# GNN setup stage: tile tables turned on TensorE and stored in one transfer, input loaded behind the weights, norms by ScalarE inside the projection

## Chip, cores and metric

One core of one Trainium2 chip. The metric is the device time of the kernel in microseconds (us), the median of the runs shown. Numbers of the profile come from one profiled execution.

## The reference

A graph network over 6,250 nodes with 128 features and 106,250 edges sorted by destination. Four layers follow each other, each with a LayerNorm and a ReLU ahead of it and a residual sum behind it. What matters here is the opening of layer 0:

```
h = relu(layer_norm(x))                        # 6250 x 128
q = typed_linear(h, node_type, Wq)             # one of 3 weight matrices per node
k = typed_linear(h, node_type, Wk) @ rel_att   # per head
v = typed_linear(h, node_type, Wv) @ rel_msg   # per head
attention over each node's incoming edges, weights exp(a - max) / sum
```

The later layers gather rows per edge and sum them per destination node (a mean, a gated sum, a mean again), and all four use the same table of edge tiles.

## The kernel before

**Tiles.** The edges, sorted by destination, are cut into T = 896 tiles of 128 (NC = 7 columns of 128 tiles each), each tile for one block of 128 nodes; the nodes fill 49 blocks, padded to NS = 50. For every tile three integers are needed later: its node block, its first edge, and the key of its last edge. They are worked out on VectorE (DVE) with tile number = partition + 128 x column and sit as three int32 arrays of 128 partitions x 7 words (`bI`, `sI`, `kI`, in OUTDEG). They go to a DRAM table `metad` of 3 x 896 words, tile after tile, and are read back from it as rows by several later loads.

**Setup, up to the projection.**

- SyncE (SP) issues the loads: one column of destinations (L834), the whole input X of 3.2 MB (L835), then 13 weight and parameter loads (L847). They are on one queue in this order.
- DVE finds the row of destinations in which each block boundary falls; GpSimd (POOL) gathers these rows (L707, 128 rows of 831 words) and DVE waits for them before L1496.
- DVE counts, ranks the blocks (L1501 to L1537), works out which tile belongs to which block (L1540 to L1561), and signals POOL, which gathers 7 source windows and 7 destination windows (L715, 14 gathers).
- DVE works out the order of turns (L1563 to L1585), masks of the node types (L1593 to L1598), copies the combined K and V weights from PSUM to W3 (L1602, L1603) and adds the FiLM row (L1604).
- DVE takes the moments of X in 50 blocks (L1404) and the factors of the norm (`spread`, L1408 to L1421, with a square root on ScalarE, ACT). Then `normalise` writes H = relu(norm(X)): 21 of the 50 blocks on ACT (L1116), 29 on DVE (L1428) with one ReLU over them (L1432). DVE waits for ACT's (L1611), then casts the gathered windows (L1614 to L1616).

**The projection** (`pe_proj`, `act_proj`, `dve_proj`, `sp_proj` with n = 0) is a pipeline over the 50 blocks. For block b DVE multiplies H by the three type masks (L532), TensorE (PE) turns the three products (L499), ACT copies them out of PSUM (L517), PE multiplies them with W3 (L506), DVE writes the queries to QT (L559) and keys and values to a staging tile STG of two slots (L526), and SP stores the slot to the table `tab2` (L592). DVE may write a slot again only when the store of two blocks earlier has landed. `pairs` (L244) lays out the steps: the first `lead` pairs of blocks and the last pair are written out, those between are a loop over a register. With n = 0 the lead is PLAN_LEAD = 15 pairs, so that blocks 0 to 29 are written out.

Other work is hung onto written-out blocks. DVE's `plan(b)` (L1618) builds the edge tables in blocks 1 to 13; PE turns 14 tiles at block 5 (L493). SP stores these tables from block 16 on, two more transfers at each of 8 blocks (`sp_tiles`, L568), then at block 24 the three arrays of `metad` (L586):

```
for k, values in ((2, kI), (0, bI), (1, sI)):
    sp.dma_start(metad[k, :].rearrange("(c p) -> p c", p=P), values)...
```

At block 28 SP waits for all of them (`tiles_stored`, STORES = 16 x 21) and loads BROW back from `metad`. POOL waits for the same count before it loads the flags (L723, L724, L727) and clears ACCR (L728). When the last store to `tab2` has landed, POOL starts the 3,520 row gathers (L691) that feed all four layers.

Of the kernel before, what the change touches and what calls it, by code (L numbers as in the profile page):

```python
# [7 lines left out]
I32 = mybir.dt.int32  # L8
# [4 lines left out]
P = 128  # L13
# [57 lines left out]
def build(nc, sz, a):  # L71
# [4 lines left out]
    with ctx:  # L76
# [167 lines left out]
        def pairs(eng, fn, trailing, lead=2):  # L244

            n = NS // 2
            for r in range(2 * lead):
                fn(r, r % 2)
            if n > lead + 1:
                with eng.Fori(lead, n - 1) as i:  # L250
                    for r in range(2):
                        fn(i * 2 + r, r)
            for r in range(2):
                fn(NS - 2 + r, r)
            for r in range(trailing):
                fn(NS + r, r)
# [94 lines left out]
        KEYS_KNOWN, WINDOWS_KNOWN, TURNS_KNOWN, SIG_IN, FILM_IN, TILES_KNOWN, TILES_MASKED = range(1, 8)  # L351
        TOTALS, ORDER_KNOWN, W_COMBINED, TILES_TURNED = range(1, 5)
# [19 lines left out]
        exp_out = sem("exp_out")  # L372
        w_free = sem("w_free")
# [10 lines left out]
        STORES = 16 * (5 + 2 * ROWS_OF)  # L384
# [29 lines left out]
        ON_ACT = (NS * 21 // 50, NS * 3 // 5, NS * 21 // 50)  # L414
# [15 lines left out]
        bI, sI, kI = (OUTDEG[:, k * NC:(k + 1) * NC].bitcast(I32) for k in range(3))  # L430
# [41 lines left out]
        PLAN_TURNED, PLAN_STORED, PLAN_LOADED = 5, 16, 28  # L472
        PLAN_LEAD = (PLAN_LOADED + 2) // 2
        TILE_ROWS = PSA[:, :, :, :].rearrange("p r j d -> p (r j d)").rearrange("p (k e) -> p k e", k=2)

# [7 lines left out]
        def pe_proj(pe, n):  # L483
# [4 lines left out]
            def step(b, r):  # L488
                if n == 0 and isinstance(b, int) and b == PLAN_TURNED:
# [4 lines left out]
                    last.then_inc(reckoned, 1)  # L494
                if has_block(b):
# [15 lines left out]
        def act_proj(act, n):  # L511
# [7 lines left out]
            pairs(act, step, 0, PLAN_LEAD if n == 0 else 2)  # L519

        def dve_proj(dve, n, plan=None):
# [457 lines left out]
        def _(pe):  # L979
# [15 lines left out]

            pe_proj(pe, 0)
# [103 lines left out]
        def _(act):  # L1100
# [68 lines left out]
            normalise(X, H, ACT.Relu)  # L1169
            act_proj(act, 0)  # L1170
# [200 lines left out]
        def _(dve):  # L1371
# [122 lines left out]

            dve.wait_ge(dst_loaded, 16)
# [24 lines left out]
            c(v_.tensor_copy(pIf, pI))  # L1520
# [19 lines left out]
            c(v_.tensor_scalar(p15, pI, GROUP - 1, None, ALU.bitwise_and))  # L1540
            c(v_.tensor_scalar(p4, pI, 4, None, ALU.logical_shift_right))
            c(v_.tensor_copy(p15f, p15))
            c(v_.tensor_copy(p4f, p4))
            c(v_.tensor_copy(grp, cI))
            c(v_.tensor_scalar(grp, grp, p4f, None, ALU.add))
            c(v_.tensor_scalar(tp, p15f, float(sz.chunk), None, ALU.mult))
            c(v_.tensor_scalar(tpos, grp, tp, None, ALU.add))
            c(v_.tensor_copy(partI, grp))
            c(v_.tensor_scalar(partI, partI, sz.chunk.bit_length() - 1, None, ALU.logical_shift_right))
            c(v_.tensor_copy(off, partI))  # L1550
            c(v_.scalar_tensor_tensor(tpos, off, float((GROUP - 1) * sz.chunk), tpos, ALU.mult, ALU.add))
# [7 lines left out]
            c(v_.tensor_copy(bI, bt))  # L1559
# [42 lines left out]
            c(v_.tensor_copy(W3[:, :, 0:D], PB[1][:, 0:3 * D].rearrange("p (t d) -> p t d", t=3)))  # L1602
# [400 lines left out]
```

## Time and profile before

| | us |
|---|---|
| median of 3 runs (5033.28 to 5042.1) | 5039.2 |
| profiled execution, its own time | 5043.33 |
| span of the profiled execution | 5041.3 |
| PE busy / DVE busy / ACT busy / POOL busy | 3019.7 / 3090.2 / 1498.2 / 3399.2 |

The span holds everything between the first and the last instruction; 2.0 us of the profiled execution lie around it. Busy times are sums over the engine's instructions. In the rows further down "L592" is line 592 of the kernel, SPq and POOLq are the queues from which these engines issue transfers, and what stands behind an arrow in brackets is what ended the idle time before an instruction.

### The profile page before, as it was taken

The numbers are of one execution on the slowest core, as the hardware profiler recorded it, in microseconds if no ns is written. First come the engines' busy times: TensorE is split into PE (matmuls) and PEld (weight loads), VectorE is DVE, ScalarE is ACT, GpSimd is POOL, SyncE is SP. The second block draws the span as 40 slices with busy tenths as digits, with TensorE's granted clock in tenths as the row PEclk, the third lists the DMA queues.
The fourth block names the chain that finished last, engine by engine and source line by source line (L and its number), as shares of the span: only waits on it lengthen the run. The fifth ranks groups of instructions, "written<-read, shape, count | busy, mean of one in ns | idle before, by whom it ended". The sixth has DMA issues, their size and how long they took to land.

```text
span 5041.3 us, 77470 instructions
## 1 busy us (share of the span) xinstructions
PE 3019.7 (60%) x15685; PEld 2533.8 (50%) x15686; DVE 3090.2 (61%) x8230; ACT 1498.2 (30%) x2837; POOL 3399.2 (67%) x3564
## 2 busy tenths in 40 slices
PE   5645555555563444455555999999996444444443
PEld 3435555454553444444443777777775434433443
DVE  6377777777777666645553777777775444444443
ACT  1123333333312000011112666666663122222222
POOL 1477777777502777777774777777774777777775
PEclk8767777777776555567775999999998555555555
DMA  2568777787811222222225767766766222222224
GB/s 75 107 171 233 226 233 224 226 230 229 209 50 45 53 53 53 53 60 66 65 66 71 189 189 185 188 186 186 187 185 106 56 56 56 56 56 56 56 56 41
DMA packets 536616, 616.11 MB, mean 122 GB/s; under 512 B 98148, under 2 KB 420751, under 8 KB 536432
## 3 DMA queue, kind: packets, MB, share of 16 engines
q0 software_dynamic: 142256, 349.44, 27.5%
q1 hardware_dynamic: 394176, 264.70, 19.8%
q14 instruction: 129, 1.06, 0.1%
q8 instruction: 55, 0.90, 0.1%
HBM read 529.54 MB, written 84.25 MB: 122 GB/s over the span
## 4 chain that ended last, share of the span: by engine, by line
POOL 43%; issue 20%; DMA 15%; DVE 10%; PE 7%; DVEq 2%; ACT 2%; SPq 1%; POOLq 0%; ACTq 0%
POOL G L691 43%; DMA G<-tab,SRC 9%; DMA mvd<-G 3%; DVE ACCR L1398 2%; PE PB L506 2%; PE PSA L902 1%; PE PB L1088 1%; DVEq L650 1%; DMA MV<-mvd 1%; PE PB L499 1%; PE PB L1026 1%; DVE ACCR L1886 1%; DMA tab<-G 1%; DVE FLG L1868 1%; ACT PB L1244 0%
## 5 line engine op out<-in xcount | busy, mean ns | idle before, releaser
L691 POOL DMA_INDIRECT G<-tab,SRC x3520 | 3360.6, 955 | 1374.1 <-issue 1042.1
L1398 DVE TENSOR_TENSOR ACCR<-ACCR,PSA 128x128 f32 (+2 forms) x3536 | 1126.9, 319 | 750.8 <-PE PSA L902 388.8
L902 PE MATMUL PSA<-G,S 128*128 128x128 f32 x3520 | 861.2, 421 | 1153.1 <-DMA G<-tab,SRC 949.2
L902 PEld LDWEIGHTS PSA<-G,S 128*128 128x128 f32 x3520 | 739.7, 311 | 1263.8 <-DVE ACCR L1398 699.7
L1381 DVE TENSOR_TENSOR S<-PB,REL 128x512 f32<-128x512 f32 x884 | 606.0, 686 | 38.3 <-DVE MASK L1450 13.7
L1026 PE MATMUL PB<-QTR,ST 128*128 x1792 | 341.3, 351 | 300.1 <-ACT ST L1207 162.3
L1026 PEld LDWEIGHTS PB<-QTR,ST 128*128 128x128 f32 x1792 | 299.9, 253 | 335.5 <-issue 334.5
L902 PE MATMUL PSA<-FLG,S 128*128 128x256 f32 x1760 | 421.8, 383 | 2.8 <-DVE FLG L1868 2.7
L902 PEld LDWEIGHTS PSA<-FLG,S 128*128 128x128 f32 x1760 | 337.3, 192 | 146.5 <-issue 91.7
L902 PE MATMUL PSA<-SCR,S 128*128 128x137 f32 x1792 | 330.7, 342 | 18.6 <-DVE ACCR L1398 18.6
L902 PEld LDWEIGHTS PSA<-SCR,S 128*128 128x128 f32 x1792 | 307.3, 248 | 23.3 <-DVE SCR L1777 23.3
L1088 PE MATMUL PB<-G,ident 128*128 128x512 f32 x440 | 245.8, 641 | 96.3 <-DMA G<-tab,SRC 86.9
L1204 ACT ACTIVATE S<-S,small 128x512 bf16<-128x512 bf16 x224 | 161.2, 720 | 372.2 <-DMA S<-relt 371.9
L1080 PEld LDWEIGHTS PB<-W,SCR 128*128 128x128 f32 x1760 | 233.1, 193 | 34.8 <-DMA SCR<-in_ea_t 22.5
L1080 PE MATMUL PB<-W,SCR 128*128 128x128 f32 x1760 | 234.1, 276 | 21.8 <-DMA SCR<-in_ea_t 21.8
L1084 PE MATMUL PB<-QTR,ST 128*128 x1760 | 234.0, 276 | 0.0
L1770 DVE TENSOR_TENSOR SCR<-G,PB 128x512 f32<-128x512 f32 x224 | 152.9, 683 | 107.7 <-issue 57.3
L1084 PEld LDWEIGHTS PB<-QTR,ST 128*128 128x128 f32 x1760 | 215.8, 193 | 0.0
L1868 DVE TENSOR_TENSOR FLG<-G,PB 128x512 f32<-128x512 f32 x220 | 149.6, 680 | 102.1 <-ACT PB L1244 98.9
L1920 DVE TENSOR_TENSOR X<-X,SCR 128x128 f32 x57 | 17.2, 302 | 310.9 <-ACT SCR L1283 310.9
L1242 ACT ACTIVATE FLG<-PB 128x512 f32<-128x512 f32 x220 | 130.2, 592 | 254.4 <-PE PB L1088 253.8
L1777 DVE TENSOR_TENSOR SCR<-MV,SCR 128x512 f32<-128x512 f32 x224 | 154.4, 689 | 75.5 <-DMA MV<-mvd 75.3
(317 smaller groups left out, 3693.0 us busy)
## 6 DMA issues: line engine op xcount, KB each, us to landing
mvd<-G SPq DMA_DIRECT2D x224, 256.0 KB, 3.4
MV<-mvd SPq DMA_DIRECT2D x224, 256.0 KB, 5.1
G<-tab,SRC POOLq DMA_INDIRECT x3520, 2.5
SCR<-in_ea_t SPq DMA_DIRECT2D x880, 64.0 KB
S<-relt SPq DMA_DIRECT2D x224, 128.0 KB
SCR<-reld SPq DMA_DIRECT2D x220, 128.0 KB
tab<-SCR SPq DMA_DIRECT2D x57, 128.0 KB, 1.7
tab<-G SPq DMA_DIRECT2D x50, 128.0 KB, 1.7
```

The source lines that it names most:

```text
L691: nc.gpsimd.indirect_dma_start(out=rows[:, slot, j, :], out_offset=None, in_=table, in_offset=bass.IndirectOffsetOnAxis(ap=SRC[:, k:k + 1] ...
L902: last = nc.tensor.matmul((PSA if banks is None else banks)[:, par, j, 0:width], S[:, slot, j, :], rhs(j), start=True, stop=True)
L1026: last = nc.tensor.matmul(QD[v % 2][:, j, :], ST[:, v % 2, j, :], QT[:, bass.ds(blocks[j], 1), :].rearrange("p o d -> p (o d)"), start=Tru ...
L1080: nc.tensor.matmul(QD[v % 2][:, j, :], EA[:, slot, j, :], W[:, 4 * D:5 * D], start=j == 0, stop=False, skip_group_check=True)
L1084: nc.tensor.matmul(QD[v % 2][:, j, :], ST[:, v % 2, j, :], QT[:, bass.ds(blocks[j], 1), :].rearrange("p o d -> p (o d)"), start=False, sto ...
L1088: nc.tensor.matmul(QD[v % 2], ident[:, :], G2[:, slot, :, 0:D], start=False, stop=True, skip_group_check=True).then_inc(s["pre_done"], 1)
L1204: nc.scalar.activation(far, far, ACT.Square, bias=minus_p).then_inc(s["far_known"], 1)
L1381: return v_.tensor_tensor(S[:, slot, :, :], bc(IOTAP, [P, QUAD, P], 1), REL[:, bass.ds(q * QUAD, QUAD)].unsqueeze(2).to_broadcast([P, QUAD ...
L1398: v_.tensor_tensor(rows, rows, banks[:, par, j, 0:width], ALU.add).then_inc(s["rows_added"], 1)
L1770: v_.tensor_tensor(PROD[:, v % 2, :, :], G2[:, slot, :, 0:D], QD[v % 2], ALU.mult).then_inc(s["multiplied"], 1)
L1777: v_.tensor_tensor(WM[:, mv % 2, :, 0:D].rearrange("p j (h d) -> p j h d", h=HEADS), MV[:, mslot, :, :].rearrange("p j (h d) -> p j h d", ...
L1868: v_.tensor_tensor(RHS[:, v % 2, :, 0:D], G2[:, slot, :, D:2 * D], GATEP, ALU.mult).then_inc(s["multiplied"], 1)
```

## The change

1. SP: the load of X moves from the front to behind the 13 loads of L847.
2. DVE: twelve small instructions on tile numbers (L1540 to L1551) and one cast (L1520) move up, to between the signal `row_known` (L1493) and the wait for the gathered rows (L1495).
3. The block and first edge of each tile are written as floats to META = ACCR[:, 576:597]; `sI` is still written as integers as well (it gives the window numbers), `bI` and `kI` are not. The key goes to META in block 9. At block 16 PE multiplies META (as the weights, 128 x 21) with the identity, which turns it to 21 rows of 128; at block 19 DVE casts them to integers in METAI (21 partitions x 128); at block 24 SP waits for that and stores it in one transfer.
4. The copies of the combined weights to W3 move from DVE to ACT, and PE waits for them ahead of the projection.
5. `normalise` is not called for layer 0's input. ACT norms four blocks ahead of the projection, and block b + 4 behind its copy of block b in each step; DVE waits for the norm of block b before L532. DVE's part of the norms, its ReLU and its wait for ACT are gone. ACT writes out the last two pairs of steps and not one.

```diff
-        def pairs(eng, fn, trailing, lead=2):
+        def pairs(eng, fn, trailing, lead=2, tail=1):
...
-        STORES = 16 * (5 + 2 * ROWS_OF)
+        STORES = 16 * (3 + 2 * ROWS_OF)
...
-        ON_ACT = (NS * 21 // 50, NS * 3 // 5, NS * 21 // 50)
+        ON_ACT = (NS, NS * 3 // 5, NS * 21 // 50)
...
-        bI, sI, kI = (OUTDEG[:, k * NC:(k + 1) * NC].bitcast(I32) for k in range(3))
+        sI = OUTDEG[:, NC:2 * NC].bitcast(I32)
+        META = ACCR[:, 576:576 + 3 * NC]
+        METAI = ACCR[0:3 * NC, 640:640 + P].bitcast(I32)
...
+        AHEAD = 4
+        META_ROWS = TILE_ROWS[0:3 * NC, 0, T:T + P]
...
+                if n == 0 and isinstance(b, int) and b == PLAN_META:
+                    pe.wait_ge(planned, TILES_MASKED)
+                    nc.tensor.matmul(META_ROWS, META, ident[:, :], start=True, stop=True).then_inc(reckoned, 1)
...
+                if n == 0 and has_block(b + AHEAD):
+                    ahead(b + AHEAD)
+            if n == 0:
+                for b in range(AHEAD):
+                    ahead(b)
+                pairs(act, step, 0, PLAN_LEAD, AHEAD // 2)
...
                 if has_block(b) and n == 0:
+                    dve.wait_ge(normed, b + 1)
...
                 if isinstance(b, int) and b == PLAN_STORED + ROWS_OF:
-                    for k, values in ((2, kI), (0, bI), (1, sI)):
-                        sp.dma_start(metad[k, :].rearrange("(c p) -> p c", p=P), values).then_inc(tiles_stored, 16)
+                    sp.wait_ge(planned, META_KNOWN)
+                    sp.dma_start(metad.rearrange("k (c p) -> (k c) p", p=P), METAI).then_inc(tiles_stored, 16)
...
-            sp.dma_start(X[:, :, :], a["x"].rearrange("(b p) d -> p b d", p=P)).then_inc(x_loaded, 16)
...
                 for dst, src in loads:
                     sp.dma_start(dst, src).then_inc(w_loaded, 16)
+                sp.dma_start(X[:, :, :], a["x"].rearrange("(b p) d -> p b d", p=P)).then_inc(x_loaded, 16)
...
+            pe.wait_ge(w_made, 2)
             pe_proj(pe, 0)
...
             nc.scalar.activation(SIG[:, 0:3], SKIP[:, 0:3], ACT.Sigmoid).then_inc(sig_out, 1)
-            normalise(X, H, ACT.Relu)
-            act_proj(act, 0)
+            act.wait_ge(reckoned, W_COMBINED)
+            for k in range(2):
+                nc.scalar.copy(W3[:, :, k * D:(k + 1) * D], PB[1 + k][:, 0:3 * D].rearrange("p (t d) -> p t d", t=3)).then_inc(w_made, 1)
+            root(st2)
+            turn_no[0] += 1
+            act.wait_ge(factors_known, turn_no[0])
+
+            def norm_row(b):
+                line = lambda tab: tab[:, bass.ds(b, 1), 0:D].rearrange("p o d -> p (o d)")
+                nc.scalar.activation(line(H), line(X), ACT.Relu, bias=st1[:, bass.ds(b, 1)],
+                                     scale=st2[:, bass.ds(b, 1)]).then_inc(normed, 1)
+            act_proj(act, 0, norm_row)
...
+            c(v_.tensor_copy(pIf, pI))
+            c(v_.tensor_scalar(p15, pI, GROUP - 1, None, ALU.bitwise_and))
...
+            c(v_.scalar_tensor_tensor(tpos, off, float((GROUP - 1) * sz.chunk), tpos, ALU.mult, ALU.add))
+
             dve.wait_ge(dst_loaded, 16)
...
-            c(v_.tensor_copy(bI, bt))
+            c(v_.tensor_copy(META[:, 0:NC], bt))
+            c(v_.tensor_copy(META[:, NC:2 * NC], st))
             c(v_.tensor_copy(sI, st))
...
             moments(X, range(NS))
             spread()
-            normalise(X, H)
-            dve.wait_ge(normed, NORMED[1])
-
             dve.wait_ge(windows_in, 32 * NC)
...
-                    c(v_.tensor_copy(kI.unsqueeze(2), KEYW[:, :, P - 1:P]))
+                    c(v_.tensor_copy(META[:, 2 * NC:3 * NC].unsqueeze(2), KEYW[:, :, P - 1:P]))
...
+                if b == 19:
+                    dve.wait_ge(reckoned, META_TURNED)
+                    c(v_.tensor_copy(METAI, META_ROWS))
+                    dve.sem_inc(planned, 1)
```

## Rows read from the trace of the kernel before

**Rows 1.** The page: span, and the chain that ended last by engine

```profile
span 5041.3 us, 77470 instructions
POOL 43%; issue 20%; DMA 15%; DVE 10%; PE 7%; DVEq 2%; ACT 2%; SPq 1%; POOLq 0%; ACTq 0%
```

**Rows 2.** Timeline of SP, POOL and DVE, 0 to 20 us: start, duration, instruction

```profile
1.35 0.94 SPq L835 DMA_DIRECT2D X<-in_x  x1
2.34 10.69 SPq L847 DMA_DIRECT2D S<-in_wk_t  x1
6.02 1.11 POOL L707 DMA_INDIRECT G<-in_dst_pm,QTR  x1 [4.18 <-DVEq L1493]
13.94 0.59 DVE L1496 CAST G<-G 128x831 f32<-128x831 int32 x1 [8.26 <-DMA G<-in_dst_pm,QTR]
...
19.51 0.44 SPq L847 DMA_DIRECT2D ROWS<-in_film_b  x1
```

**Rows 3.** Window gathers of L715: times from issue to landing

```profile
DMA to landing us min/median/max: 2.4/3.8/7.7
```

**Rows 4.** Timeline of DVE, ACT and POOL, 25 to 66 us

```profile
25.22 0.15 DVE L1540 TENSOR_SCALAR QTR<-QTR 128x1 int32<-128x1 int32 x1
...
27.71 0.52 DVE L1552 TENSOR_TENSOR QTR<-QTR 128x350 f32<-128x350 f32 x1
...
39.22 0.56 DVE L1602 COPY W<-PB 128x384 f32<-128x384 f32 x1
...
40.41 0.42 DVE L1604 TENSOR_TENSOR ROWS<-ROWS,PB 128x256 f32<-128x256 f32 x1
40.86 9.76 DVE L1404 BATCH_NORM_STATS2 ACCR<-X 128x6 f32<-128x128 f32 x50
...
48.62 0.94 POOL L715 DMA_INDIRECT G<-in_dst_win,QTR  x1 [0.30 <-issue]
...
53.38 8.18 ACT L1116 ACTIVATE H<-X,st 128x128 f32<-128x128 f32 x21 [0.84 <-DVEq L1421]
53.44 7.52 DVE L1428 TENSOR_SCALAR H<-X,st 128x128 f32<-128x128 f32 x29 [0.15 <-DVE st L1420]
...
63.12 0.63 DVE L1614 CAST SCR<-G 128x896 f32<-128x896 int32 x1
...
65.23 1.03 DVE L532 TENSOR_TENSOR G<-H,MASK 128x384 f32<-128x384 f32 x2 [0.15 <-DVE ACCR L1616]
```

**Rows 5.** Timeline of the projection, 126 to 156 us

```profile
126.03 1.73 SPq L587 DMA_DIRECT2D metad<-OUTDEG  x3
...
129.66 2.10 PE L506 MATMUL PB<-W,G 128*128 128x384 f32 x6
...
131.92 2.10 PE L506 MATMUL PB<-W,G 128*128 128x384 f32 x6
...
148.57 0.42 DVE L526 TENSOR_SCALAR G<-PB 128x256 f32<-128x256 f32 x1 [16.48 <-DMA tab<-G]
...
153.81 2.10 PE L506 MATMUL PB<-W,G 128*128 128x384 f32 x6
```

**Rows 6.** The three stores of L587: issue to landing

```profile
DMA to landing us min/median/max: 10.4/20.5/21.2
```

**Rows 7.** Transfers issued up to 330 us: size, median us to landing

```profile
reld<-G SPq DMA_DIRECT2D x8, 28.0 KB, 1.9
```

**Rows 8.** Stretch 131 to 149 us: engines' busy time, PEclk, DMA share, GB/s

```profile
131.00:149.00 18.00, 3.02 (x12) 1.56 (x10) 0.72 (x3) 0.48 (x1) 0.35 (x1) 0.73 0.91 13
```

**Rows 9.** Waits up to 290 us: total, times, longest

```profile
POOL G L691 <- DMA tab<-G: 36.1, 1, 36.1
...
DVE G L526 <- DMA tab<-G: 18.8, 3, 16.5
```

**Rows 10.** Instruction groups of ACT up to 290 us: busy, mean ns, idle before

```profile
L517 ACT COPY G<-PB 128x384 f32<-128x384 f32 x50 | 24.0, 480 | 113.1 <-PE PB L499 113.1
...
L1108 ACT ACT_TABLE_LOAD x1 | 1.3, 1283 | 0.0
```

More of the change, by code:

```diff
@@ L248, in pairs @@
                 fn(r, r % 2)
-            if n > lead + 1:
-                with eng.Fori(lead, n - 1) as i:
+            if n > lead + tail:
+                with eng.Fori(lead, n - tail) as i:
                     for r in range(2):
                         fn(i * 2 + r, r)
-            for r in range(2):
-                fn(NS - 2 + r, r)
+            for r in range(2 * tail):
+                fn(NS - 2 * tail + r, r % 2)
             for r in range(trailing):
@@ L350, in build @@
         windows_in = sem("windows_in")
-        KEYS_KNOWN, WINDOWS_KNOWN, TURNS_KNOWN, SIG_IN, FILM_IN, TILES_KNOWN, TILES_MASKED = range(1, 8)
-        TOTALS, ORDER_KNOWN, W_COMBINED, TILES_TURNED = range(1, 5)
+        KEYS_KNOWN, WINDOWS_KNOWN, TURNS_KNOWN, SIG_IN, FILM_IN, TILES_KNOWN, TILES_MASKED, META_KNOWN = range(1, 9)
+        TOTALS, ORDER_KNOWN, W_COMBINED, TILES_TURNED, META_TURNED = range(1, 6)
         turns_in = sem("turns_in")
@@ L372, in build @@
         exp_out = sem("exp_out")
+        w_made = sem("w_made")
         w_free = sem("w_free")
@@ L470, in proj_sems @@
             return s
-        PLAN_TURNED, PLAN_STORED, PLAN_LOADED = 5, 16, 28
+        PLAN_TURNED, PLAN_META, PLAN_STORED, PLAN_LOADED = 5, 16, 16, 28
         PLAN_LEAD = (PLAN_LOADED + 2) // 2
         TILE_ROWS = PSA[:, :, :, :].rearrange("p r j d -> p (r j d)").rearrange("p (k e) -> p k e", k=2)
+        AHEAD = 4
+        META_ROWS = TILE_ROWS[0:3 * NC, 0, T:T + P]
         proj = [proj_sems(n) for n in ("typed_qkv", "typed_out")]
@@ L509, in pe_proj, with act_proj @@
             pairs(pe, step, 1, PLAN_LEAD if n == 0 else 2)
-        def act_proj(act, n):
+        def act_proj(act, n, ahead=None):
             s, (ni, w, cols) = proj[n], proj_w[n]
@@ L518, in step @@
                                PB[r][:, 0:ni * P]).then_inc(s["copied"], 1)
-            pairs(act, step, 0, PLAN_LEAD if n == 0 else 2)
+                if n == 0 and has_block(b + AHEAD):
[4 more added lines that the diff above has]
+                pairs(act, step, 0, PLAN_LEAD, AHEAD // 2)
+            else:
+                pairs(act, step, 0)
         def dve_proj(dve, n, plan=None):
@@ L1493, in _ @@
             dve.sem_inc(row_known, 1)
+            c(v_.tensor_copy(pIf, pI))
+            c(v_.tensor_scalar(p15, pI, GROUP - 1, None, ALU.bitwise_and))
+            c(v_.tensor_scalar(p4, pI, 4, None, ALU.logical_shift_right))
+            c(v_.tensor_copy(p15f, p15))
+            c(v_.tensor_copy(p4f, p4))
+            c(v_.tensor_copy(grp, cI))
+            c(v_.tensor_scalar(grp, grp, p4f, None, ALU.add))
+            c(v_.tensor_scalar(tp, p15f, float(sz.chunk), None, ALU.mult))
+            c(v_.tensor_scalar(tpos, grp, tp, None, ALU.add))
+            c(v_.tensor_copy(partI, grp))
+            c(v_.tensor_scalar(partI, partI, sz.chunk.bit_length() - 1, None, ALU.logical_shift_right))
+            c(v_.tensor_copy(off, partI))
+            c(v_.scalar_tensor_tensor(tpos, off, float((GROUP - 1) * sz.chunk), tpos, ALU.mult, ALU.add))
             dve.wait_ge(dst_loaded, 16)
@@ L1537, in _ @@
             c(v_.tensor_tensor(delta[:, 1:NE], rel0[:, 1:NE], rel0[:, 0:NE - 1], ALU.subtract))
[L1540 to L1551, printed above, removed]
             c(v_.tensor_tensor(M, bc(cum, [P, NC, NE], 1), tpos.unsqueeze(2).to_broadcast([P, NC, NE]), ALU.is_le))
@@ L1601, in _ @@
             dve.wait_ge(reckoned, W_COMBINED)
-            c(v_.tensor_copy(W3[:, :, 0:D], PB[1][:, 0:3 * D].rearrange("p (t d) -> p t d", t=3)))
-            c(v_.tensor_copy(W3[:, :, D:2 * D], PB[2][:, 0:3 * D].rearrange("p (t d) -> p t d", t=3)))
             c(v_.tensor_tensor(ROWS[:, 3:5, :].rearrange("p a d -> p (a d)"), ROWS[:, 3:5, :].rearrange("p a d -> p (a d)"),
```

1 line of the change is left out of this document (removed).

## Prediction

> **What bounds the kernel now.** I read the page first, for the size of things: over the span of 5041.3 us the chain that ended last is mostly POOL [rows 1], the row gathers of the four layers, and the change touches none of them. So the question is when the first of these gathers can start, and whether what follows merely moves with it. POOL is ready long before: it sits idle for 36.1 us until the last store to the table has landed [rows 9]. The end of the projection sets it, and behind that lies one serial path, which I then followed in the timeline. It has three pieces. (1) DVE's stream from the boundary rows to the first masked block, 65.23 us [rows 4], nearly without a gap but for 8.26 us in which it waits for the gathered rows [rows 2]. (2) The projection at PE's pace: two neighbouring steps start at 129.66 and 131.92, 2.26 us apart [rows 5]. (3) A hole in it: DVE cannot refill a staging slot for 16.48 us, until 148.57, since a store to the table has not landed [rows 5].
>
> What the hole waits for is seen from two sides. The three stores of L587 took 10.4 to 21.2 us to land [rows 6], though they carry 3.5 KB each, while a store of 28 KB from the same queue takes 1.9 us [rows 7]. In that stretch the transfer engines are busy for 0.91 of the time and move 13 GB/s [rows 8]: 2,688 single words, one after the other, with the table's stores queued behind them.
>
> **The change part by part.** Durations and sum refer to the profiled execution, 5043.33 us with 2.0 us around its span; it is 4.1 us above the median of 5039.2, and I take the same difference off both.
>
> *X behind the weights.* Today X (3.2 MB) is in flight from 1.35 us, the first weight load is held in issue for 10.69 us, and the last is issued at 19.51 [rows 2]. The gather of boundary rows, issued at 6.02, lands 7.9 us later among this traffic. With X last, the weights take some 8 us to issue (the other twelve took 13.03 to 19.95 us, and the first should be like its neighbour), so that X leaves at about 9.5 us, when the gather is nearly in. The window gathers, of a sixth of the size, took 2.4 to 7.7 us, 3.8 at the median [rows 3]. These are my ends: below by 2.4, above by the present 7.9. I take 4.5 (the median, and something for the size): DVE goes on at 10.5 and not 13.94, minus 3.4 us. X itself needed 15.6 us at most of flight and would be in by 25 us; DVE asks for it at about 34. It costs nothing; with that cover gone, each us later than 34 would cost one.
>
> *Thirteen instructions moved up.* L1540 to L1551 take from 25.22 to 27.71 [rows 4], 2.5 us, and L1520 one more step of 0.2: 2.7 us leave the chain. In their new place they run from 5.8 to 8.5 us, inside the wait for the gather. This is also a floor: however fast the gather is, DVE does not go on before 8.5, so the first term can be 5.4 at most. One more copy (first edges both as float and as integer) costs 0.2. Net minus 2.5.
>
> *W3 copied by ACT.* L1602 to L1604 start 1.19 us apart [rows 4]: minus 1.2. ACT has nothing else to do then, and PE needs W3 only at the projection, some 15 us later.
>
> *Norms.* With 7.1 us saved so far the moments start at 33.8 and the factors are ready at 46.4 (53.44 before). From there to L1614 at 63.12 is 9.7 us of norm, ReLU and wait [rows 4], which leave DVE's path. What is late next is the windows: their gathers start 5.9 us earlier (they do not profit from the W3 copies), so the last is issued at 42.7 and not 48.62 [rows 4] and lands, at the median of 3.8 [rows 3], at 46.5. DVE's casts thus start at 46.5 or 46.6. ACT's four norms ahead take 4 x 0.39 us (21 in 8.18 [rows 4]), 1.6 us, beside DVE's casts of 2.1. The first masked block comes at 48.7 and not 65.23: **minus 16.5** for all parts together up to here. The ends are minus 12 (gather unchanged, windows 1 us late) and minus 18.5.
>
> Inside the projection ACT has 2.26 us a step, of which its copy takes 0.48 [rows 10]. A norm of 0.48 brings it to 0.96. The norm stands behind the copy that PE waits for and four blocks ahead of its use. Cost zero, hidden in ACT's idle time. What the register addresses of the 16 rolled steps cost on ACT no row shows: below nothing is excluded, above it is free up to the slack of 1.3 us a step. I take 0.
>
> Here a rule speaks against the change. DVE does 29 blocks in 7.52 us with 2.1 for their ReLU, 0.33 a block, and ACT 0.39 [rows 4]; ACT is the slower engine for it. The Trainium skill (ScalarE: Activation LUTs, Rules for kernel authors) says to put ReLU and multiplications on VectorE and not on ScalarE. By it, 50 blocks ahead of the loop would cost 19.5 us of ACT against 9.7 now; that this kernel places all but four under PE's steps is what the rule leaves out.
>
> *One store in place of three.* The hole: from 131.92 to 153.81 PE gets two steps done in 21.89 us, where 4.53 are due. It costs 17.4 us [rows 5], of which 16 are the wait and the rest PE restarting at a lower clock (0.73 granted in the stretch [rows 8]). The 2,688 words become 21 rows of 512 bytes. I price their landing by the 28 KB store, 1.9 us [rows 7], no more than the other stores of these blocks, which stop nobody. Added is one turn on PE, the engine that sets the pace: six passes of 384 columns take 2.10 us [rows 5], 0.35 each, so two passes of 128 columns cost between 0.1 and 0.7, I take 0.4; and one cast on DVE, hidden in its wait for PE. SP's new wait at block 24 has only table stores behind it, and DVE signals in block 19: nothing. What stays is the flags' traffic: of DVE's three waits on the table's stores (18.8 us) the other two are 2.3 [rows 9]. POOL will issue these loads earlier, but as before inside the projection, so I leave them as they are; they may cost up to 3 us more or 1 less. **Minus 17.0.**
>
> *Sum:* 16.5 + 17.0 = 33.5. 5043.3 becomes 5009.8 in a profiled execution, and the median 5039.2 becomes 5005.7. Everything behind the projection starts 33.5 us earlier and depends on nothing with a time of its own: POOL will have cleared its flags and ACCR some 36 us ahead of need, as now.
>
> **The rivals.**
>
> *The hole stays.* If the table's stores were held not by the single words but by the backlog of the 17 transfers of blocks 16 to 23, or the flags' loads took the place of the words, some 16.5 us remain: 5022. For it speaks only that these come together; against it, that each of the 28 KB stores landed in 1.9 us until the single words came. 5 in 100.
>
> *No change.* Layer 0 could be paced by something that does not move, and take back what is given. The wait of 36.1 us [rows 9] says that POOL hangs on the table alone. Time 5035 to 5043. 4 in 100.
>
> *Slower, by ACT's tables.* ReLU and copy now alternate on ACT, 50 times. If each change of function needed a table, at 1283 ns a load [rows 10], a step would take 0.96 + 2 x 1.28 = 3.5 us of ACT, over PE's 2.26: 50 x 1.25 = 62 us lost, 33 gained, 5068. The point at which this turns to a loss is 2.93 us a step. Against it: in the first 290 us, where 21 ReLUs are followed by 50 copies, the square root's table is the only one loaded after the sigmoid's [rows 10]. The Trainium skill (ScalarE: Activation LUTs, Table sets) says that relu and copy are in every set; its price for a switch, about 2.7 us, would give 120 us more. 2 in 100.
>
> **How the numbers follow.** 0.2%, about 10 us, is what a measurement can tell from no change. The forecast has 88 in 100, the rivals 5, 4 and 2, one is left for a loss of another kind. Within the forecast the ends are minus 12 and minus 18.5 for the first part, minus 13.5 and minus 18 for the second, and the runs themselves spread over 9 us: 5006 becomes 4996 to 5018. I take the upper end to 5020. Faster 0.93, same 0.04, slower 0.03.
>
> **What would show it.** L1496 at 10 to 11 us, L1404 at about 34, L1614 at 46 to 47 with windows or DVE as its releaser, the first L532 at 48.7. ACT's steps with a copy and a norm, no table load between. The store to metad landing in about 2 us, PE's steps 2.26 us apart through blocks 24 to 30, no wait of L526 over 3 us, the first L691 at 171 to 173. The forecast is wrong if the first L691 is later than 180, or if it is not, and the span is still less than 25 us shorter.

## The result, and the profile after

The changed kernel takes 5006.8 us, the median of 4 runs (5003.98 to 5009.44). The kernel before takes 5039.4 us beside it (5033.28 to 5042.1). The ratio is 0.9933 with an interval of 0.9918 to 0.9948, 32.6 us less. The profiled execution took 5007.18 us around a span of 5005.4.

First the page, to see whether anything changed behind the setup. Span and chain:

```profile
span 5005.4 us, 77541 instructions
POOL 44%; issue 20%; DMA 15%; DVE 9%; PE 7%; DVEq 2%; ACT 2%; SPq 1%; POOLq 0%; ACTq 0%
```

The chain is the one of [rows 1], 35.9 us shorter. So I followed the serial path again. The timeline of SP, POOL, DVE and ACT, 6 to 51 us (start, duration, instruction, idle time before it and what ended it):

```profile
6.02 1.11 POOL L724 DMA_INDIRECT G<-in_dst_pm,QTR  x1 [4.19 <-DVEq L1521]
...
8.15 0.87 SPq L864 DMA_DIRECT2D X<-in_x  x1
...
8.48 0.17 DVE L1535 SCALAR_TENSOR_TENSOR QTR<-ACCR,QTR 128x7 f32<-128x7 f32 x1
12.74 0.59 DVE L1538 CAST G<-G 128x831 f32<-128x831 int32 x1 [4.09 <-DMA G<-in_dst_pm,QTR]
...
36.03 9.76 DVE L1432 BATCH_NORM_STATS2 ACCR<-X 128x6 f32<-128x128 f32 x50
...
44.98 0.94 POOL L732 DMA_INDIRECT G<-in_dst_win,QTR  x1 [0.30 <-issue]
...
48.56 1.65 ACT L1196 ACTIVATE H<-X,st 128x128 f32<-128x128 f32 x4 [0.84 <-DVEq L1449]
48.61 0.63 DVE L1639 CAST SCR<-G 128x896 f32<-128x896 int32 x1
...
50.71 1.03 DVE L549 TENSOR_TENSOR G<-H,MASK 128x384 f32<-128x384 f32 x2 [0.15 <-DVE ACCR L1641]
```

Against [rows 2, 4]: DVE goes on behind the gather at 12.74 (13.94 before), starts the moments at 36.03 (40.86), casts the windows at 48.61 (63.12) and makes the first masked block at 50.71 (65.23). The part up to there is 14.5 us shorter. Two details count later. The small instructions end at 8.65 and DVE still waits 4.09 us for the gather. And no bracket stands behind L1639: the windows were there, DVE itself was the last to arrive.

Then the projection, in the timeline of PE, DVE, SP and POOL from 90 to 129 us, and POOL's first row gather:

```profile
90.46 0.40 PE L503 MATMUL PSA<-ident,ACCR 128*21 128x128 f32 x2
...
112.45 0.38 SPq L604 DMA_DIRECT2D metad<-ACCR  x1
...
114.15 0.64 POOL L740 DMA_DIRECT2D FLG<-flagd  x1 [68.23 <-DMA metad<-ACCR]
...
116.09 2.10 PE L515 MATMUL PB<-W,G 128*128 128x384 f32 x6
...
118.35 2.10 PE L515 MATMUL PB<-W,G 128*128 128x384 f32 x6
...
125.16 2.10 PE L515 MATMUL PB<-W,G 128*128 128x384 f32 x6
...
127.17 0.42 DVE L542 TENSOR_SCALAR G<-PB 128x256 f32<-128x256 f32 x1 [1.74 <-DMA tab<-G]
...
128.90 2.10 PE L515 MATMUL PB<-W,G 128*128 128x384 f32 x6
...
174.68 1.03 POOL L708 DMA_INDIRECT G<-tab,SRC  x1 [39.98 <-DMA tab<-G]
```

The hole of [rows 5] is gone. The store to `metad` is issued at 112.45, and at 114.15 POOL passes its wait for it: it landed in 1.7 us at most, where the three stores took 10.4 to 21.2 [rows 6]. PE's steps stay 2.26 us apart (116.09, 118.35), but for one pair, 125.16 to 128.90, 1.48 us over the pace. The first row gather starts at 174.68 and not 205.26: 30.6 us earlier.

ACT's groups up to 290 us (busy, mean ns, idle before):

```profile
L1196 ACT ACTIVATE H<-X,st 128x128 f32<-128x128 f32 (+1 forms) x50 | 24.4, 494 | 0.8 <-DVEq L1449 0.8
...
L526 ACT COPY G<-PB 128x384 f32<-128x384 f32 x50 | 24.0, 479 | 76.0 <-PE PB L508 76.0
...
L1126 ACT ACT_TABLE_LOAD x1 | 1.3, 1283 | 0.0
```

POOL still waits for the table alone, 39.98 us before its first row gather. ACT does all 50 norms and idles 76.0 us over the 50 copies (113.1 in [rows 10]). ACT changes from copy to ReLU and back fifty times, and no further table load appears. DVE waits for stores to the table four times, 2.9 us in all, the longest 1.7 (three times and 18.8 in [rows 9]).

### The profile page after: what moved, and what is told of

Read it like the earlier page. It is cut to its first block, busy times and chain, and to the rows that moved or that the text cites. A ratio compares the mean times of both kernels' runs of the same rounds, so it can differ in the third digit from the quotient of the medians.

```text
span 5005.4 us, 77541 instructions
## 1 busy us (share of the span) xinstructions
PE 3026.9 (60%) x15687; PEld 2538.2 (51%) x15688; DVE 3080.3 (62%) x8200; ACT 1509.9 (30%) x2868; POOL 3394.4 (68%) x3564
## 4 chain that ended last, share of the span: by engine, by line
POOL 44%; issue 20%; DMA 15%; DVE 9%; PE 7%; DVEq 2%; ACT 2%; SPq 1%; POOLq 0%; ACTq 0%
POOL G L708 44%; DMA G<-tab,SRC 10%; DMA mvd<-G 3%; DVE ACCR L1426 3%; PE PB L515 2%; PE PSA L919 1%; PE PB L1106 1%; DVEq L667 1%; PE PB L508 1%; DVE ACCR L1915 1%; DMA MV<-mvd 1%; SPq L791 1%; DVE FLG L1897 1%; ACT PB L1272 0%; ACT L1143 0%
```

## The experiments

Three things were to be found out: whether the parts of the change add up as the sum says; what holds the gather of boundary rows, which was far from the forecast; and how near ACT is to setting the pace. The kernels ran in three groups of four, each group on one chip and beside the kernel before on that chip. I compare the time from the start of the span to the first row gather of layer 0, and the median against that of the kernel before in the same group. The kernel before was only timed in the groups: its first row gather is always the 205.26 us of its own profile, and that of the changed kernel the 174.68 above, but for the third group. The totals named in the expectations start from 5039 us, and the kernel before is 7.7 us faster on the first group's chip; so for the totals I compare differences. "The first chip" is the one of the changed kernel's own runs; its trace is the one read above.

### First group: the parts alone (before: 5031.7 us, 16 runs, 5026.88 to 5035.3)

**Words.** The three columns are stored as single words again, everything else is as changed:

```diff
-                    sp.wait_ge(planned, META_KNOWN)
-                    sp.dma_start(metad.rearrange("k (c p) -> (k c) p", p=P), METAI).then_inc(tiles_stored, 16)
+                    for k, values in ((2, kI), (0, bI), (1, sI)):
+                        sp.dma_start(metad[k, :].rearrange("(c p) -> p c", p=P), values).then_inc(tiles_stored, 16)
```

> The changed kernel with the three stores of single words put back (no turn on PE, no METAI). Theory (the words hold the table's stores behind them): DVE waits some 16 us for a staging slot around block 24, the first row gather of layer 0 starts 16 to 18 us later than in the changed kernel (174.7 there), near 191.5, and the whole time rises by as much, to about 5023. Rival (the backlog of the 17 other transfers is the cause): the wait is as short as in the changed kernel and the time moves by less than 3 us.

Measured: first row gather at 190.0 us, 15.3 later than with the change; median 5018.4 (5016.79 to 5028.45), ratio 0.9977 (0.9967 to 0.9987). The wait and its length, in the waits and in the timeline:

```profile
DVE G L539 <- DMA tab<-G: 17.8, 3, 15.0
```

```profile
111.84 1.25 SPq L601 DMA_DIRECT2D metad<-OUTDEG  x2
...
132.45 0.42 DVE L539 TENSOR_SCALAR G<-PB 128x256 f32<-128x256 f32 x1 [15.03 <-DMA tab<-G]
132.54 0.64 POOL L737 DMA_DIRECT2D FLG<-flagd  x1 [86.75 <-DMA metad<-OUTDEG]
```

(Two of the three stores are in this row; the first was issued at 111.36.) The hole is back, at its new place in time, and the moments start within 0.2 us of where they did. That refutes the rival by which the backlog of the other stores makes the hole: that backlog is the same with and without the words. DVE's wait for the table's store ends within 0.1 us of POOL's wait for the words, so the stores behind the words land when the words do. Whether the table's stores would be held as well if they went by another queue (the transfer engines themselves are 0.91 busy in the hole, [rows 8]) no run tried.

**Only meta.** The kernel before with part 3 of the change alone (the same turn, cast and single store).

> The kernel before with only the tile tables turned on PE and stored in one transfer. Theory (terms add): the hole of 17.4 us goes, 0.4 us of PE is added, the flags' waits stay, so the first row gather of layer 0 starts at 188 to 189 (205.3 before) and the total is 5022 to 5023. Rival (layer 0 takes back or adds a part of what setup gains): the gather starts there, but the total differs from 5022.5 by more than 5 us.

Measured: first row gather at 189.1, 16.2 us earlier than before; median 5016.0 (5010.41 to 5019.46), 15.7 less, ratio 0.9968 (0.9955 to 0.998). Put back or taken out alone, the words are worth 15.3 and 16.2 us, so they hardly depend on the other parts.

**Norms ahead.** The norms go back to before the projection, 21 blocks on ACT and 29 on DVE:

```diff
-        ON_ACT = (NS, NS * 3 // 5, NS * 21 // 50)
+        ON_ACT = (NS * 21 // 50, NS * 3 // 5, NS * 21 // 50)
...
-            act_proj(act, 0, norm_row)
+            normalise(X, H, ACT.Relu)
+            act_proj(act, 0)
...
             spread()
+            normalise(X, H)
+            dve.wait_ge(normed, NORMED[1])
```

> The changed kernel with all norms ahead of the projection again, 21 blocks on ACT and 29 on DVE. Theory (norms are free under PE's steps, and cost 9.7 us of DVE's path when ahead): first masked block at 60.4 and not 50.7, first row gather at 184.4, total about 5016.5. Rival (norms on ACT cost PE something in each step, so that part of the gain is paid back): the steps of the projection become shorter here, and the first row gather comes less than 8 us later than in the changed kernel.

Measured: the casts at 58.36 and not 48.61, first row gather at 185.0, 10.3 later; median 5013.0 (5007.26 to 5013.76), ratio 0.996 (0.9946 to 0.9974). The timeline, 48 to 60 us:

```profile
48.62 8.18 ACT L1126 ACTIVATE H<-X,st 128x128 f32<-128x128 f32 x21 [0.84 <-DVEq L1434]
48.67 7.53 DVE L1441 TENSOR_SCALAR H<-X,st 128x128 f32<-128x128 f32 x29 [0.15 <-DVE st L1433]
...
58.36 0.63 DVE L1626 CAST SCR<-G 128x896 f32<-128x896 int32 x1
```

The 9.7 us between 48.67 and 58.36 are the term of the sum, to a tenth. The other 0.6 us of the 10.3 are lost inside the projection, where PE's first steps take 0.1 us more (14.2 from its first turn to its turn of block 5, and 14.0 with the change) and the steps around the flags' loads 0.4 more.

**X at the front.** The load of X goes ahead of the weights again, everything else is as changed.

```diff
+            sp.dma_start(X[:, :, :], a["x"].rearrange("(b p) d -> p b d", p=P)).then_inc(x_loaded, 16)
             loads = [
...
-                sp.dma_start(X[:, :, :], a["x"].rearrange("(b p) d -> p b d", p=P)).then_inc(x_loaded, 16)
```

> The changed kernel with the load of X in front of the weights again. Theory (X in flight is what slows the gather of boundary rows, though it gained only 1.2 us and not 3.4): DVE goes on after the gather at 13.9 and not 12.7, everything behind comes 1.2 us later, first row gather near 175.9, total within 3 us of the changed kernel. Rival (the order of the loads is without effect on the gather): it lands at the same time, 12.7, or earlier.

Measured: the cast of the gathered rows at 14.04 and not 12.74, the moments at 37.3, the first masked block at 52.0, each 1.3 us later. But the first row gather starts at 174.4, 0.3 earlier than with the change and 1.5 earlier than expected, and the median is 5001.4 (4999.61 to 5003.45), ratio 0.9941 (0.9925 to 0.9958). So the 1.3 us were real and lost again within the projection. The 1.6 us went in two places. From PE's first turn to its turn of block 5 pass 13.2 us here and 14.0 with the change (52.73 to 65.96, 51.42 to 65.45). And DVE's waits for the table's stores sum to nearly the same (2.8 and 2.9 us) but are at most 1.3 us long and not 1.7, so that PE loses 0.7 us of its pace there and not 1.5. That neither has to do with X is my reading: both lengths also vary among versions that load X at the same place (see "What was not expected"). The interval of the ratio overlaps that of the change: moving X is worth 1.3 us at the gather and nothing that a run of the whole kernel can show.

Put together, in us:

| | first row gather, earlier than before by | median, less than before by |
|---|---|---|
| only meta | 16.2 | 15.7 |
| words (all but meta) | 15.2 | 13.3 |
| norms ahead | 20.3 | 18.7 |
| X at the front | 30.9 | 30.3 |
| the change (its own runs) | 30.6 | 32.6 |

What is gained at the first row gather arrives at the end within 2 us in each. No run speaks for the rival by which layer 0 takes it back. The expectation of the only-meta run had set that rival a limit, a total more than 5 us away from 5022.5. The 5016.0 lie 6.5 under it, but this chip's kernel before is 7.7 us faster, so the theory's total would be 5014.8 here, and the limit is not passed.

### Second group: what holds the gather, and ACT's limit (before: 6281.9 us, 7 runs)

This chip runs every kernel about 25% slower behind the setup, the kernel before included. The setup itself is the same to about 2 us (DVE idles 1.2 to 1.9 us between the moments and the factors here, where it did not on the first chip), so its times may be compared with those above, and the medians only within the group.

**X after the gather.** SP waits for the gathered rows before it issues X, so that X and the gather can't meet:

```diff
+                sp.wait_ge(dst_loaded, 16)
                 sp.dma_start(X[:, :, :], a["x"].rearrange("(b p) d -> p b d", p=P)).then_inc(x_loaded, 16)
```

> The changed kernel with the load of X held until the gather of boundary rows has landed. Theory A (X, issued at 8.15 while the gather is in flight, is what keeps it at 6.6 us): the gather lands in about 4.5 us, DVE goes on at 10.5, the first row gather starts near 172.5, 2.2 us earlier; X lands by 28 us, and DVE asks for it at 34, so nothing is lost. Theory B (the weights in flight, or the gather's own size, set the 6.6 us): it lands at 12.4 to 12.7 as in the changed kernel and nothing moves.

**Loads after the gather.** The same wait, ahead of the 13 weight loads (X stays behind them):

```diff
             with nc.allow_non_contiguous_dma(reason="columns of a few words"):
+                sp.wait_ge(dst_loaded, 16)
                 for dst, src in loads:
```

> The changed kernel with weights and X all held until the gather has landed. Theory A (X alone): as with X alone held. Theory B1 (weights in flight): the gather lands 1 to 3 us sooner than with X alone held. Theory B2 (its own size, 128 rows of 3.3 KB): still 6 us or more with nothing else in flight.

The gather of boundary rows, issue to landing, in the changed kernel, with X after the gather, and with all loads after it:

```profile
DMA to landing us min/median/max: 6.6/6.6/6.6
```

```profile
DMA to landing us min/median/max: 6.2/6.2/6.2
```

```profile
DMA to landing us min/median/max: 4.0/4.0/4.0
```

X at the front gives 7.9, as the kernel before. So without X the gather gains 0.4 us more, and without the weights another 2.2: theory A is refuted, and of theory B it is the weights in flight (B1) that hold the gather, not its size. DVE then goes on at 12.3 and 10.1, and the moments start at 35.6 and 33.4. The first row gather starts at 175.7 and 173.2, and not near the 172.5 of theory A; the idle time of this chip ahead of the factors is in both. What the forecast took for a gather among little traffic, 4.5, is nearly the time without any, 4.0. The median with X after the gather is 6241.6 (ratio 0.9939, 0.9923 to 0.9956), and the single run with all loads after it took 6236.7.

**ACT with more to do.** Ahead of each norm ACT makes one more pass, over 512 or 2048 columns of X into a tile that is not in use yet, and waits for it:

```diff
+                nc.scalar.activation(MV[:, :, :, :].rearrange("p r j d -> p (r j) d")[:, 0:4, :], X[:, 0:4, :], ACT.Relu).then_inc(extra, 1)
+                act.wait_ge(extra, b + 1)
                 nc.scalar.activation(line(H), line(X), ACT.Relu, bias=st1[:, bass.ds(b, 1)],
```

> The changed kernel with one more ACT pass over 512 columns ahead of each norm, into a tile unused at that time: about 0.7 us more for ACT in each of 50 steps, 1.7 of 2.26 us. Theory (ACT has slack and the norm stands behind the copy that PE waits for): PE's steps stay 2.26 us apart, the first row gather comes 2 to 3 us later, for the four passes ahead of the projection alone. Rival (ACT is close to being the bound): PE's steps grow, and the first row gather comes over 10 us later.

> The same with a pass over 2048 columns, about 2.0 us more in each step: ACT needs some 3.0 us and PE 2.26. Theory: ACT sets the pace, steps of 2.9 to 3.2 us, the first row gather 40 to 50 us later, and the total up by as much. This is the point at which norms inside the projection would turn to a loss. Rival (norms four blocks ahead hide it still): less than 20 us.

The timelines of PE and ACT with 512 columns, then with 2048:

```profile
82.57 2.10 PE L516 MATMUL PB<-W,G 128*128 128x384 f32 x6
82.77 0.48 ACT L527 COPY G<-PB 128x384 f32<-128x384 f32 x1 [0.73 <-PE PB L509]
83.14 0.63 ACT L1197 ACTIVATE MV<-X 128x512 f32<-128x512 f32 x1
83.81 0.49 ACT L1199 ACTIVATE H<-X,st 128x128 f32<-128x128 f32 x1
84.83 2.10 PE L516 MATMUL PB<-W,G 128*128 128x384 f32 x6
```

```profile
84.41 0.46 ACT L527 COPY G<-PB 128x384 f32<-128x384 f32 x1
84.77 1.91 ACT L1197 ACTIVATE MV<-X 128x2048 f32<-128x2048 f32 x1
84.92 2.20 PE L516 MATMUL PB<-W,G 128*128 128x384 f32 x6 [0.17 <-ACT G L527]
86.71 0.49 ACT L1199 ACTIVATE H<-X,st 128x128 f32<-128x128 f32 x1
87.11 0.46 ACT L527 COPY G<-PB 128x384 f32<-128x384 f32 x1
...
87.62 1.56 PE L516 MATMUL PB<-W,G 128*128 128x384 f32 x4 [0.17 <-ACT G L527]
```

With 512 columns ACT has 0.73 us left in a step and PE keeps its 2.26: first row gather at 175.6, 0.9 later than with the change on the first chip and not 2 to 3 (6249.9 us in its single run). With 2048 the releaser turns round. PE waits for ACT and a step takes 2.70 us (84.92 to 87.62): first row gather at 200.2, 25 us later than with 512 (6270.5 us in its single run). That is the direction expected and about half the size. The reason stands in the rows: from start to start the three instructions need 0.36, 1.94 and 0.40, together 2.70, though their durations sum to 2.86: the extra pass and the copy start 0.1 us before the instruction ahead of them is shown to end, while the norm, which waits for the extra pass, starts 0.03 behind its end. DVE's waits for the table's stores also shrink, to 0.9 us. So the norm of 0.49 us is free here. With the 0.63 us of the small pass and the 0.73 us left beside it, ACT has room for some 1.4 us more work in each step before it costs anything (my estimate from these rows).

### Third group: a version with the loads late, and the terms that were left (before: 6278.6 us, 14 runs, 6264.52 to 6311.86)

This chip is as slow as that of the second group. **The change again** is the changed kernel word for word, as the control of this group.

> The changed kernel once more, as a control. Theory (what setup gains goes through one to one, and what is beyond it in a single pair of profiles is scatter): the first row gather starts 30 to 31 us earlier than the 205.3 of the profile before, and the whole time is 29 to 33 us under that of the kernel before on the same chip, where the first pair of profiles lay 36 apart. Rival (the stages behind the projection gain another 5 us): 35 to 37.

Measured: first row gather at 176.5; median 6244.5 (6232.64 to 6258.92), 34.1 less than before, ratio 0.9947 (0.9929 to 0.9965). The interval reaches from 22 to 45 us. It holds the 30.6 us of the first row gather, and would also hold a good part of what its rival gave, so this run alone decides nothing. One thing in its trace was not there on the first chip, a wait of DVE between moments and factors that the profile puts down to nothing on this core:

```profile
48.52 0.24 DVE L1439 TENSOR_TENSOR st<-ACCR 128x50 f32<-128x50 f32 x1 [2.22 <-remote]
```

With it the casts start 2.7 us later than on the first chip, and 0.9 of these are won back in the projection, so that the first row gather is 1.8 later. The idle time lies in the traces of this group with lengths of 0.8 to 2.2 us, which blurs their comparisons by as much.

**Loads late** is the kernel with all loads behind the gather once more, run several times, as the version that may beat both.

> The kernel loads_after_gather once more, on the chip of the control. Theory (the weights in flight, not X, hold the gather of boundary rows): the gather lands 4.0 us after its issue, DVE goes on at 10.1, the first row gather starts 1.5 to 2.5 us earlier than in the control, and the total is 1.5 to 2.5 us lower, less than a measurement tells. Rival (weights that come later are missed at PE or DVE): the gain is gone before the first masked block.

Measured: the gathered rows at 10.1, the moments at 33.4, the first row gather at 171.9, 4.6 us before the control. Of these, 2.7 are the gather's, 0.9 the control's longer gap ahead of the factors (casts at 47.6 and 51.3), and the last 0.9 are won in the projection, 0.8 of them in PE's first steps (13.1 us from its first turn to its turn of block 5, and 13.9 in the control) and 0.1 around the flags' loads. That is more than the 1.5 to 2.5 expected, and only the 2.7 are known to come from the edit. The median is 6235.4 without one run of 7588.74 us, which I set aside as an outlier, and the ratio 0.9929 (0.9908 to 0.9951). That median is 9.0 us under the control's, but the interval overlaps the control's by about half: this version is the earliest of all at the first row gather, and its whole time is not shown to be lower.

**Flags later.** POOL clears ACCR before it loads the flags, which moves these loads back by the 10.8 us of the clearing:

```diff
             pool.wait_ge(tiles_stored, STORES)
+            nc.gpsimd.memset(ACCR[:, :], 0.0).then_inc(acc_cleared, 1)
+            pool.wait_ge(acc_cleared, 1)
...
-            nc.gpsimd.memset(ACCR[:, :], 0.0).then_inc(acc_cleared, 1)
```

> The changed kernel with POOL clearing ACCR (10.8 us) ahead of the loads of the flags and not behind them. Theory (the flags' loads are what leaves DVE 2.9 us of waits on the table's stores): these waits move from 121 to 129 us to 132 to 140 us, their sum stays between 2 and 4 us. Rival (they come from the stores of the tables, of the meta rows or from the load of BROW): they stay at 121 to 129 us.

The timeline of POOL and DVE, 115 to 141 us:

```profile
115.51 10.77 POOL L737 MEMSET ACCR<- 128x12800 f32 x1 [69.57 <-DMA metad<-ACCR]
126.58 0.64 POOL L742 DMA_DIRECT2D FLG<-flagd  x1 [0.30 <-POOL ACCR L737]
...
135.23 0.42 DVE L542 TENSOR_SCALAR G<-PB 128x256 f32<-128x256 f32 x1 [1.40 <-DMA tab<-G]
...
136.89 0.42 DVE L542 TENSOR_SCALAR G<-PB 128x256 f32<-128x256 f32 x1 [0.57 <-DMA tab<-G]
...
140.77 0.42 DVE L542 TENSOR_SCALAR G<-PB 128x256 f32<-128x256 f32 x1 [1.66 <-DMA tab<-G]
```

In the control DVE's three waits for the table's stores stand at 126.7, 128.9 and 131.7 and sum to 2.9 us. Here the first is 8.5 us later, the last 9.1, and they sum to 3.6; around 127 to 132 us, where the control has them, DVE doesn't wait. So the flags' loads make these waits whenever they come, and moving them within the projection saves nothing: the first row gather starts at 176.6, with 176.5 in the control. The single run took 6238.8 us.

**The small parts back.** The thirteen instructions go behind the wait for the gathered rows, and the copies to W3 back to DVE:

```diff
+            dve.wait_ge(dst_loaded, 16)
+            c(v_.tensor_copy(DSTF, DSTI))
             c(v_.tensor_copy(pIf, pI))
...
-            dve.wait_ge(dst_loaded, 16)
-            c(v_.tensor_copy(DSTF, DSTI))
...
+            c(v_.tensor_copy(W3[:, :, 0:D], PB[1][:, 0:3 * D].rearrange("p (t d) -> p t d", t=3)))
+            c(v_.tensor_copy(W3[:, :, D:2 * D], PB[2][:, 0:3 * D].rearrange("p (t d) -> p t d", t=3)))
```

> The changed kernel with the thirteen small instructions behind the wait for the gather again, and the two copies to W3 on DVE. Theory (both lie on DVE's serial path): moments 4.0 us later than in the changed kernel (2.8 for the instructions, 1.2 for the copies), at 40.0, the first row gather at about 178.7, total up by 4. Rival (the windows' gathers or ACT take up the difference): less than 2.5 us at the first masked block.

Measured: the moments start at 39.88 against 36.11 in the control, 3.8 us later, and the first row gather at 179.5, 3.0 later. In between, DVE's idle time ahead of the factors is 2.2 us in the control and 0.8 here, which leaves 2.6 us at the first masked block (56.01 and 53.41). The median, 6246.0 (6234.92 to 6249.87, ratio 0.9939, 0.9917 to 0.9962), is not told from the control's. The two terms are on the path as the sum says; the kernel's whole time can't resolve them.

## Why the prediction was right, and where a term was not

The forecast was 5006 us, and 5006.8 came. The sign and the mechanism held. The steps one by one:

- **What bounds it.** The first row gather hangs on the last store to the table and on nothing else (POOL's wait, 40.0 us), and five versions pass what they gain there on to the end within 2 us. That refutes the rival "no change".
- **One store in place of three, −17.0.** Measured from the first masked block to the first row gather: 140.0 us before, 124.0 after, −16.1. The hole is worth what was said, and the turn on PE took the 0.40 us put down for it. Two small things make up the rest: DVE's waits during the flags' loads cost PE 1.48 us in one step where they had cost 1.15 over three, and PE took 0.5 us more from its first turn to its turn of block 5 (14.0 against 13.6). One reading of the forecast is loose: it takes the lower clock after the hole from the 0.73 of the stretch 131 to 149, which lies before PE starts again. The granted clock of 149 to 152 is 0.50, and the six passes of that step take 3.43 us and not 2.10, so what it concludes holds. That the words, and not the backlog, held the table's stores is shown by the two runs that change only them. The Trainium skill (DMA: Bandwidth & Descriptors, Rules for kernel authors) says that a strided last dimension becomes one descriptor for each element, and to rearrange so that it is contiguous. The landings agree: 2,688 single words took up to 21.2 us, the same data in 21 rows 1.7 at most.
- **Norms, −9.7.** Measured 9.7: from the start of the moments to the casts, 22.3 us before and 12.6 after. Putting them back alone moves the casts by 9.7 and the first row gather by 10.3.
- **Windows late next.** Wrong in kind, harmless in size. The forecast let the last window land at 46.5, with DVE's casts at 46.5 or 46.6, a near tie. POOL issued the last one at 44.98, 2.3 us later than forecast, and DVE came 2.1 later, at 48.61. That would still be a near tie with the 3.8 us taken for the landing; the casts found the windows there, so the last one landed in 3.6 us or less.
- **Small instructions and W3, −2.5 and −1.2.** DVE started the moments 4.8 us earlier, of which the gather is 1.2, so that the two are 3.6 together; alone, put back on another chip, 3.8.
- **The gather, −3.4.** This is the term that was mis-sized: it measured −1.2. The step that failed is "X leaves at about 9.5 us, when the gather is nearly in", and with it the choice of 4.5 us among ends of 2.4 and 7.9. X left at 8.15, sooner than forecast, and the gather landed 6.6 us after its issue at 6.02. The forecast had put down the 7.9 us of before to X alone and priced the gather without it almost unladen. But the same change that takes X from in front of the weights lets the weights run beside the gather: they are issued from 1.20 us on and not held behind X. The gather landed in 6.6 us among them, in 6.2 with X kept away altogether, and in 4.0 only with the weights away too. The 6.6 us lie between the ends of 2.4 and 7.9; the value taken between them should have been near the upper one.
- **ACT's cost in the loop, 0.** Right, with 76.0 us of idle time over 50 blocks left. The rival of the tables is refuted: there is no load between 50 ReLUs and 50 copies. (The 120 us that it adds for a dearer switch should be about 140 by its own figures.) When ACT is made to set the pace, a step takes the time from start to start of its instructions, 2.70 us, and not the sum of their durations.

The setup therefore gave 30.6 us and not 33.5: 2.2 are missing at the gather and 0.9 in the projection, and the windows, put down for 0.2, cost nothing. The median nevertheless came within about 1 us of the forecast. The medians lie 32.6 apart, 2.0 more than the first row gathers, and the two profiled executions 36.2, since the time behind the first row gather was 4830.7 us in this profile and 4836.0 in that of before. No part of the change acts there, and the runs of one kernel spread over 5 to 9 us, so these 5 us are scatter between executions. That the whole was hit more closely than its parts is luck of that size. This is also the limit of the experiments: terms of 1 to 4 us are shown at the place where they act and not in the whole time.

## What to carry to other kernels

Where a serial path ends in one wait, measure each part of a change at the next few points along that path, since there a single profile resolves tenths of a microsecond, where the whole time resolves only several. Compare just behind the place where the part acts: here two stretches of the projection vary by 1.2 and 1.3 us among the versions, with no edit made to them that explains it. When a big load is moved away from in front of a small urgent one, price the small one among what then takes its place and not alone. And look for stores of single words on a queue that something in a hurry also uses: here DVE waited 15.0 to 16.5 us for a table store that stood behind them.

## What was not expected of the hardware

**How far other traffic slows one gather.** The same gather of 128 rows took 4.0 us with all loads held back, 6.2 to 6.7 among the weights and 7.9 with the 3.2 MB of X ahead of them. The step from nothing to the weights, 2.2 us, is larger than that from the weights to X, 1.2 to 1.7.

**ACT's instructions overlap.** Where one does not wait for the one ahead of it, it starts about 0.1 us before the end that the profile shows for that one (84.77 and 87.11 above); where it waits for it, it does not (86.71). So a loop of three needs 2.70 us and not 2.86.

**PE's first steps don't follow the granted clock in the profile.** A table of stretches (length, then busy time of PE, PEld, DVE, ACT and POOL with their counts, PEclk, DMA share, GB/s), with PE's first rows in the timeline behind it (L508 turns, L515 multiplies with W3), first of the changed kernel, then with X at the front:

```profile
51.00:54.00 3.00, 2.58 (x8) 1.98 (x9) 2.78 (x5) 1.63 (x4) 0.00 (x0) 1.00 0.00 0
```

```profile
51.42 1.51 PE L508 MATMUL PB<-ident,G 128*128 128x128 f32 x6 [17.18 <-DVE G L549]
52.86 4.21 PE L515 MATMUL PB<-W,G 128*128 128x384 f32 x6
```

```profile
51.00:54.00 3.00, 1.27 (x6) 1.14 (x6) 2.81 (x5) 0.87 (x3) 0.00 (x0) 0.50 0.00 0
54.00:57.00 3.00, 3.00 (x7) 1.61 (x6) 1.15 (x3) 1.27 (x4) 0.00 (x0) 0.50 0.00 0
```

```profile
54.17 3.63 PE L515 MATMUL PB<-W,G 128*128 128x384 f32 x6
```

The first starts its projection at 51.42 with the full clock granted (2.4 GHz) and needs 14.0 us to its turn of block 5; the second starts at 52.73 with half of it (1.2 GHz) granted until 57 and needs 13.2. PE had idled for 17 us before either. The pace itself is slow in both: the six turns take 1.51 us and the six passes 4.21 and 3.63, where six turns take 0.98 and six passes 2.10 later on. It looks as if PE ran at half clock in both and the first trace does not show it, but no run tested that. In all versions but the one with 2048 columns this stretch takes 13.0 to 14.2 us, and what PE loses around the flags' loads 0.7 to 1.9 us; what sets either length is open.

**Chips differ.** The kernel before took 6282 and 6279 us on the chips of the second and third group, against 5032 on that of the first and 5039 beside the changed kernel's own runs, with its setup the same to about 2 us. In the stretch from 195 to 1350 us, the changed kernel in its own runs and on the third group's chip:

```profile
195.00:1350.00 1155.00, 653.24 (x3641) 590.25 (x3642) 864.03 (x1999) 369.51 (x821) 845.86 (x864) 0.72 0.78 220
```

```profile
195.00:1350.00 1155.00, 470.87 (x2653) 429.07 (x2653) 629.24 (x1442) 267.17 (x600) 641.70 (x663) 0.67 0.60 166
```

The second moves 166 GB/s where the first moves 220. A row gather keeps POOL as long on either (951 and 953 ns), but POOL stands idle before them for 2610 us in all and not 1379. The cause is open too. One more thing differs: in the whole trace of the changed kernel on the third group's chip the engines wait 385 times, 2310 us summed over them, for something that the profile finds nowhere on this core ("remote"), and in that of its own runs never. It doesn't touch the ratios, which compare kernels on one chip.
